# Order of the weight loads of the first feed-forward pass, and place of one masked softmax part, in an audio-tower kernel on Trainium2

## What is computed

```python
h = tok(x, W, b)                               # 64 x 10 patches of 128 samples -> 640 tokens of 512
h = h + attn(layernorm(h), Wq, Wk, Wv, Wo)     # per batch row: 10 positions, 16 heads of 32
h = h + ffn(layernorm(h), w_gate_up, w_down)   # silu(gate) * up, inner width 2048
# attn, with s = 10 positions:
scores = q @ k.T / sqrt(32) + causal
heavy  = argmax over keys of sum over queries of softmax(scores)   # heavy budget int(0.1 * 10) = 1
scores = where(heavy | (abs(i - j) <= 1), scores, lowest)
out    = softmax(scores) @ v @ Wo.T
```

## Time and profile before

| | |
|---|---|
| median of 3 runs | 268.63 us (267.5 to 268.77) |
| the profiled execution's own time | 268.19 us |
| its span, first to last instruction | 266.4 us |
| PE busy | 257.1 us, 96% |
| DVE busy | 169.9 us, 64% |
| ACT busy | 108.2 us, 41% |
| POOL busy | 48.9 us, 18% |
| DMA | 38.61 MB, mean 145 GB/s |

### The profile page before, as it was taken

How to read it: one execution, slowest core, us unless ns; L and a number is a source line. 1 busy time by engine, 2 the same in 40 slices (tenths; PEclk the granted TensorE clock), 3 DMA queues, 4 the chain that set the end, 5 groups by cost and what they waited for, 6 DMA issues and landing times.

```text
span 266.4 us, 5045 instructions
## 1 busy us (share of the span) xinstructions
PE 257.1 (96%) x1909; PEld 213.5 (80%) x1909; DVE 169.9 (64%) x333; ACT 108.2 (41%) x181; POOL 48.9 (18%) x53
## 2 busy tenths in 40 slices
PE   7999999799999999989999999999999999999993
PEld 5466498575887887867888879999999999999992
DVE  1696998997899987899976775633333333343323
ACT  2311212863285454749531053533443333344320
POOL 0116032004001121100100101422222222222210
PEclk9999999999999999999999999999999999999999
DMA  6996003005359999983890050694333344400004
GB/s 220 416 418 220 1 4 122 2 2 100 59 161 232 290 252 288 271 270 135 219 285 12 0 198 5 168 336 127 119 118 118 118 121 126 128 19 0 0 0 118
DMA packets 13154, 38.61 MB, mean 145 GB/s; under 512 B 1864, under 2 KB 1936, under 8 KB 12496
## 3 DMA queue, kind: packets, MB, share of 16 engines
q1 hardware_dynamic: 11120, 32.17, 35.2%
q0 software_dynamic: 1728, 5.81, 11.5%
q10 hardware_dynamic: 288, 0.39, 0.4%
HBM read 31.24 MB, written 1.31 MB: 122 GB/s over the span
## 4 chain that ended last, share of the span: by engine, by line
PE 78%; DMA 8%; DVE 6%; ACT 3%; issue 3%; SPq 1%; POOL 0%; DVEq 0%; POOLq 0%
PE ps L225 49%; PE ps L1345 5%; PE ps L1223 5%; PE ps L1118 4%; DMA wgu<-stage 3%; PE ps L1326 3%; DMA stage<-w_ffn 3%; PE ps L1238 3%; PE ps L1185 3%; PE ps L1144 2%; DMA dims<-w_dims 2%; PE ps L1127 1%; PE ps L1069 1%; PE ps L1155 1%; DVE xT L724 1%
## 5 line engine op out<-in xcount | busy, mean ns | idle before, releaser
L225 PE MATMUL ps<-xT,wgu 128*128 128x384 f32 x384 | 70.5, 339 | 0.2 <-DVE gu L931 0.2
L225 PEld LDWEIGHTS ps<-xT,wgu 128*128 128x128 f32 x384 | 68.1, 188 | 1.8 <-issue 0.6
L931 DVE TENSOR_TENSOR gu<-silu,ps 128x256 f32<-128x256 f32 (+1 forms) x32 | 15.5, 485 | 47.5 <-PE ps L225 44.4
L363 POOL TENSOR_TENSOR wd<-stage,wd 128x512 fp32r<-128x512 f32 x16 | 26.2, 1636 | 77.1 <-ACT wd L431 77.1
L225 PE MATMUL ps<-wd,hT 128*128 128x512 f32 x156 | 38.8, 393 | 0.0
L591 ACT ACTIVATE silu<-ps 128x256 f32<-128x256 f32 (+1 forms) x32 | 14.0, 437 | 52.7 <-PE ps L225 52.2
L225 PEld LDWEIGHTS ps<-wd,hT 128*128 128x128 f32 x156 | 29.0, 188 | 5.4
L225 PE MATMUL ps<-xs,wgu 128*128 128x256 f32 x240 | 31.9, 289 | 0.9 <-DMA wgu<-stage 0.9
L225 PEld LDWEIGHTS ps<-xs,wgu 128*128 128x128 f32 x240 | 28.8, 188 | 4.6 <-issue 4.1
L431 ACT ACTIVATE wgu<-stage 128x1024 fp32r<-128x1024 f32 x20 | 21.1, 1056 | 24.4 <-PE ps L225 23.1
L1345 PE MATMUL ps<-stage,gu 128*128 128x512 f32 x56 | 26.3, 593 | 0.0
(11 more groups left out here) (126 smaller groups left out, 318.3 us busy)
## 6 DMA issues: line engine op xcount, KB each, us to landing
stage<-w_ffn SPq DMA_DIRECT2D x32, 512.0 KB, 4.5
stage<-w_ffn SPq DMA_DIRECT2D x32, 256.0 KB, 4.0
wgu<-stage POOLq DMA_DIRECT2D x6, 512.0 KB, 8.3
wd<-stage POOLq DMA_DIRECT2D x3, 512.0 KB, 7.0
stage<-w_k SPq DMA_DIRECT2D x1, 1024.0 KB, 6.6
stage<-w_q SPq DMA_DIRECT2D x1, 1024.0 KB, 10.1
stage<-w_v SPq DMA_DIRECT2D x1, 1024.0 KB, 12.1
wo<-w_o SPq DMA_DIRECT2D x1, 1024.0 KB, 15.2
```

The source lines that it names most:

```text
L225: ins = pe.matmul(dst, lhs[a], rhs[b], start=first and n == 0, stop=last and n == 2)
L363: pool.tensor_tensor(dst, src, f32(hi), ALU.subtract).then_inc(done, 1)
L931: dve.tensor_tensor(gu[:, ring, cols], silu[:, ring, cols], ps[:, up, at:at + P * TILES[p]], ALU.mult)\
```

## The change

Three places. SP issues the gate/up loads of blocks 6 and 7 ahead of those of blocks 4 and 5, and each W_down load up to block 12 stands two steps later in its list against the gate/up loads. ACT runs `hi_attn(0)` ahead of `minus_weights(2)` instead of behind it. DVE makes only the mask of softmax step 3 ahead of `softmax_out(2)`; the three other instructions of `softmax_in(3)` come behind the value products of queries 7, 6, 5 and 4, and `statistics(3)` goes ahead of `softmax_out(3)`. ACT's `exponential(3)` stays where it was, ahead of the six drains.

```diff
             next_gate_up / next_down (SP)
+            next_gate_up(2)
+            next_gate_up(3)
             next_gate_up(0)
-            for i in range(1, NB):
+            next_gate_up(1)
+            next_down(0)
+            for i in range(4, S2 + 1):
+                next_gate_up(i)
+                next_down(i - 3)
+            next_gate_up(S2 + 1)
+            next_down(S2 - 2)
+            next_down(S2 - 1)
+            next_down(S2)
+            for i in range(S2 + 2, NB):
                 next_gate_up(i)
                 next_down(i - 1)
             next_down(NB - 1)
@@ scalar
             act.activation(warm[:, :], neghalf[:, :], ACT.Silu)
+            hi_attn(0)
             minus_weights(2)
-            hi_attn(0)
             hi_attn(1)
@@ vector
-            def softmax_in(n):
+            def softmax_in(n, unmasked=True):
                 g, masked, part = SOFTMAX[n]
                 if masked:
-                    mask(part)
+                    if unmasked:
+                        mask(part)
@@ vector
             softmax_in(2)
-            softmax_in(3)
+            mask(SOFTMAX[3][2])
             softmax_out(2)
             values(0, 7, 6, 5, 4)
+            softmax_in(3, unmasked=False)
+            statistics(3)
             softmax_out(3)
             values(0, 3, 2, 1, 0)
-            statistics(3)
             statistics(4)
```

## The result

| | before | changed |
|---|---|---|
| median, same runs | 268.7 us (6 runs, 267.5 to 271.71) | 274.07 us (6 runs, 273.53 to 274.94) |
| ratio | | 1.0205, 95% interval 1.0165 to 1.0246 |
| profiled execution: own time, span | 268.19, 266.4 us | 274.4, 272.6 us |

The changed kernel is slower by 2%, 5.4 us. The time is inside the forecast's range, but it is not the likeliest case's 271.8 us: it is that of the first rival, the clock that falls. The range holds it because that rival's price was put into it.

What follows compares the result with a forecast made beforehand. PE was taken to bound the kernel, busy 257.1 of 266.4 us. Own time 268.19 + 4.1 (delay) - 0.9 (low part) = 271.4 us, with 0.44 for the median 271.8 us; range 270.9 to 274.6.

Steps and rivals of the forecast that it cites:

- likeliest case: Whole kernel: PE starts its value sums later but keeps full clock, and a low-part wait goes; 271.8 us, chance 0.47.
- first rival: PE's value sums: clock falls to half in the 5.5 us idle time, costing 1.5 to 2.4 us; 273.3 to 274.2 us, chance 0.38.
- The wait that goes, and the one that takes its place: Ahead of PE's first value sums: 0.88 us saved on DVE, but PE idles 5.5 us in place of 1.43.
- The delay of 4.1 us: PE's first value sums start at 57.25 in place of 53.16 us, waiting for ACT's drains behind DVE's difference.
- The loads: SP's gate/up loads of blocks 6 and 7 go out early, near 67 and 73 us, at no cost, freeing a crowded stretch.
- the term of 0.9 us: PE's wait for block 10's low weight part, in the window of 80 to 117 us, goes entirely; bounds 0 and 0.9.
- W_down later: W_down loads placed later in SP's queue still arrive before PE's down matmuls: cost nothing, margin over 4 us.
- `hi_attn(0)`: On ACT, moved ahead of block 2's negated weight copy: costs nothing, cover over 11 us, gains nothing against the trace.
- The faster rival: PE's first value sums depend on DVE's product alone, not held by ACT's drains: 266.8 us, chance 0.04.

Runs made afterwards that it cites:

- table-first kernel: Changed kernel with ACT's exponential(3) behind the six drains, hi_attn(0) left behind the Silu table load: 269.18 us, ratio to before 1.0013.
- the filler: Changed kernel with 20 matmuls whose result nobody reads on PE ahead of the value sums: 272.0 us, ratio to before 1.0109.
- loads alone: Kernel before with only SP's new order of loads: 268.27 us, ratio to before 0.9981.
- softmax part alone: Changed kernel with SP's old order of loads, so the softmax edit and hi_attn(0) only: 274.41 us, ratio to before 1.0207.
- drains-first kernel with the old loads: Changed kernel with exponential(3) behind the six drains, hi_attn(0) ahead of the Silu table load, SP's old load order: 268.35 us, ratio to before 0.9989.
- drains-first kernel: Changed kernel with exponential(3) behind the six drains and hi_attn(0) ahead of the Silu table load: 267.62 us, ratio to before 0.9974.
- one product, 7 fillers: Changed kernel with step 3's difference behind one value product, not four, plus 7 unread matmuls in PE's idle time: 269.31 us, ratio to before 1.0034.
- one product, 3 fillers: Changed kernel with step 3's difference behind one value product, not four, plus 3 unread matmuls in PE's idle time: 271.31 us, ratio to before 1.0096.
- one product: Changed kernel with step 3's difference behind one value product (query 7) in place of four: 271.8 us, ratio to before 1.0114.
- two products: Changed kernel with step 3's difference behind two value products (queries 7 and 6) in place of four: 272.77 us, ratio to before 1.0157.

## Why the prediction was right or wrong

- **The wait that goes, and the one that takes its place: right.** The forecast had PE's sums start 5.5 us after it stopped, the trace has 5.59; it had an idle time of ACT of about 6 us, the trace has 6.05. The delay of 4.1 us is 4.16. Each link was then moved by itself: the number of products ahead of the difference (waits of 2.98 and 4.00 us), and the place of ACT's exponential against the drains (0.67 us in the table-first kernel).
- **The likeliest case: wrong.** The step that failed is the choice between forecast and first rival. I gave 0.47 to a clock that stays, on the ground that 5.5 us lay between an idle time of 1.43 us, which kept it, and the start of the program. In all six runs the mean granted clock is 0.984 to 0.987, where the 59 runs of the kernel before beside the experiments have 0.990 to 1.000: it fell every time. The price was bounded at 1.5 to 2.4 us from the first matmuls of the program; it was 2.25 in the profile (5.31 against 3.06 us with the filler), 2.1 by the filler in medians. The forecast also had the sums take 3.28 us "and no less"; with all products ready and the clock at full they take 3.06. The rival's 273.3 to 274.2 us holds the measured 274.07. The Trainium skill (TensorE: Matmul & The Clock Gate, the table under "Why this matters for your kernels") warns of gaps over about 3 us; the traces agree for 5.6 and 4.0 us, and go beyond it: at 2.98 and 2.12 us the clock fell too, so for this kernel the limit to keep is the measured one.
- **The loads: right in kind, too large in size.** SP's two early loads went out well ahead of the others, as forecast, only some 3 us later than forecast, as `minus_weights(2)` stands behind the slowed value sums. The changed kernel's SP issues (start, us; the last line holds two):

```profile
69.91 0.33 SPq L301 DMA_DIRECT2D stage<-w_ffn  x1
...
76.46 0.33 SPq L301 DMA_DIRECT2D stage<-w_ffn  x1
...
81.69 2.11 SPq L301 DMA_DIRECT2D stage<-w_ffn  x2
```

  The accumulating DMA of block 10 fell from 9.13 to 6.1 us (loads alone). But the term of 0.9 us was the wait of one execution. By the starts of the down matmuls each of the four profiles with the old order loses 0.5 to 1.4 us here (1.12 and 0.67 before, 0.53 with the softmax part alone, 1.36 in the drains-first kernel with the old loads). Of the nine with the new order eight lose nothing; the filler kernel loses 0.47 us, behind an accumulating DMA of 9.1 us. In times the order is worth less than can be told: 0.5 us alone, 0.3 in the changed kernel (medians), 0.4 in the drains-first one, each within its interval. Why the gain in time is smaller than the waits that go is open.
- **W_down later: right.** No run with the new order shows a wait of PE at the down matmuls for a load, and but for the filler kernel they follow each other every 4.46 us from 103 to 128 us.
- **`hi_attn(0)`: right for the kernel as changed.** PE has no wait for it in the changed kernel's list. No run moved this one instruction alone in the kernel before. That ACT's order there can matter is shown by the 1.4 us of the table-first kernel.
- **The faster rival: out.** PE did depend on the third drain. What this rival described is the drains-first kernel, at 267.62 us where 266.8 was worked out; DVE's order ahead of the first norm and the smaller size of the low part's term stand against the rest.

## What to carry to other kernels

When a step that passes through two engines is moved, move both halves: an instruction that stays in its place on the second engine becomes a wait for the new place on the first, and everything behind it in that in-order list is late with it. So before moving DVE's part of a softmax, list what stands behind its exponential on ACT and who waits for that. And price an idle gap of TensorE twice, once as the gap and once as the half-speed stretch that follows: here 4.2 and 2.3 us (5.31 against 3.06). And read a stage's waits from the starts of its instructions as well as from the list of waits: the list missed one of 0.5 us.

## What the runs showed of the hardware

The granted clock fell in much shorter idle times than I had expected. PE's idle time, and when the clock went to half after PE had stopped (from the mean clock of one-microsecond windows, in the changed kernel of one of three, as each has two levels only):

| kernel | idle, us | clock fell after | first value sums |
|---|---|---|---|
| one product, 7 fillers | 1.23 | stayed | 3.06 us |
| before | 1.43 | stayed | 3.28 us |
| one product, 3 fillers | 2.12 | 2.1 us | 4.66 us |
| one product | 2.98 | 2.1 us | 5.81 us |
| two products | 4.00 | 1.6 us | 5.17 us |
| changed | 5.59 | 3.5 us | 5.31 us |
| softmax part alone | 5.60 | 2.7 us | 4.94 us |

The window for the last row:

```profile
55.00:56.00 1.00, 0.00 (x0) 0.00 (x0) 1.00 (x3) 0.00 (x0) 0.00 (x0) 0.66 0.00 0
```

The time from the stop to the fall is not the same each time: the last two rows have the same work and idle time, and 0.8 us between them. It was as short as 1.6 us, so an idle time a little under 2.1 us may not be safe either; nothing between 1.43 and 2.12 us was run. "Stayed" is said of the profiled executions. Of the ten runs of the kernel with 7 fillers one has a mean clock of 0.990 and is the slowest (271.07 us), and of 59 of the kernel before two have 0.990 and 0.992; where it fell in these isn't on record. A few matmuls on constants, put into the gap, kept the clock: 20 of them were worth 2.1 us in the changed kernel, 7 were worth 2.1 to 2.5 us in the one-product kernel. In the changed kernel they did not move the start of the value sums (58.11 against 58.08), and what they needed was a PSUM bank that was free.
